# Expert stages of a two-layer gated cross-attention model: inner weights of groups 1 to 7 loaded in place, their low parts on GpSimd

## The reference

```python
# layer 0: E = 4 experts, D = 512, F = 2048, top 2 of 4
h = silu(einsum('td,edf->etf', xf, w1)) * einsum('td,edf->etf', xf, w3)
out = einsum('te,etd->td', gates, einsum('etf,efd->etd', h, w2))
# layer 1: E = 8 experts, D = 512, H = 1024, top 2 of 8
h1 = einsum('bsd,hd->bsh', x, W1[e]); h2 = einsum('bsd,hd->bsh', x, W2[e])
y = einsum('bsh,dh->bsd', h1 * sigmoid(h1) * h2, W3[e])
out = out + y * w_e[..., None]          # for e in range(8)
```

## Time and profile before

| | us |
|---|---|
| median of 3 runs (2252.22 to 2254.47) | 2253.94 |
| the profiled execution | 2267.11 |
| its span | 2265.1 |
| busy: PE / PEld / DVE / ACT / POOL | 1964.1 / 1589.4 / 1071.3 / 851.7 / 585.7 |

### The profile page before, as it was taken

How to read it: one execution, slowest core, us unless ns; L and a number is a source line. 1 busy time by engine, 2 the same in 40 slices (tenths; PEclk the granted TensorE clock), 3 DMA queues, 4 the chain that set the end, 5 groups by cost and what they waited for, 6 DMA issues and landing times. The chain is left out here.

```text
span 2265.1 us, 35412 instructions
## 1 busy us (share of the span) xinstructions
PE 1964.1 (87%) x12328; PEld 1589.4 (70%) x12328; DVE 1071.3 (47%) x2316; ACT 851.7 (38%) x1791; POOL 585.7 (26%) x479
## 2 busy tenths in 40 slices
PE   5799999999999999996699999999758667887883
PEld 3478777777878787875577877777537556776772
DVE  6325555555555555444544333333256644454444
ACT  3234343434434343343433333333134434444440
POOL 3030202020111111000433333434402044455453
PEclk9899999999999999998799999999878778999997
DMA  8620111010101020000433223333480333344445
GB/s 206 211 83 27 29 33 34 27 40 9 58 8 58 9 58 8 17 16 31 158 94 111 84 80 97 110 99 106 175 265 8 132 111 116 121 148 142 123 126 191
DMA packets 112954, 201.48 MB, mean 89 GB/s; under 512 B 32568, under 2 KB 33368, under 8 KB 112300
## 3 DMA queue, kind: packets, MB, share of 16 engines
q1 hardware_dynamic: 107196, 178.88, 26.0%
q0 software_dynamic: 4800, 15.73, 2.0%
q10 hardware_dynamic: 816, 5.05, 0.6%
HBM read 171.64 MB, written 27.98 MB: 88 GB/s over the span
## 5 line engine op out<-in xcount | busy, mean ns | idle before, releaser
L458 POOL TENSOR_TENSOR a_rows<-a_rows,a_gain_x 128x512 f32<-128x512 f32 (+1 forms) x48 | 68.2, 1420 | 555.4 <-DVE a_rows L873 555.4
L1090 PE MATMUL f_banks<-f_wab_hi,f_x_hi 128*128 x448 | 187.7, 419 | 18.0 <-DVE f_wab_lo L1670 10.8
L617 PE MATMUL a_kv_ps<-a_kvin_hi,a_wk_hi 128*128 128x512 f32 (+1 forms) x512 | 196.2, 383 | 1.0 <-DVE a_kvin_lo L880 1.0
L1090 PE MATMUL m_banks<-m_wab_hi,m_x_hi 128*128 x512 | 164.9, 322 | 36.6 <-DVE m_wab_lo L1670 24.5
L618 PE MATMUL a_kv_ps<-a_kvin_lo,a_wk_hi 128*128 128x512 f32 (+1 forms) x512 | 180.4, 352 | 0.0
L619 PE MATMUL a_kv_ps<-a_kvin_hi,a_wk_lo 128*128 128x512 f32 (+1 forms) x512 | 180.3, 352 | 0.0
L1092 PE MATMUL f_banks<-f_wab_hi,f_x_lo 128*128 x448 | 178.2, 398 | 0.0
L1091 PE MATMUL f_banks<-f_wab_lo,f_x_hi 128*128 x448 | 177.1, 395 | 0.0
L1709 DVE TENSOR_TENSOR f_h_sb<-f_h_sb,f_banks 128x256 f32<-128x256 f32 x112 | 47.2, 421 | 262.3 <-ACT f_h_sb L1445 258.9
L540 ACT ACTIVATE a_probs<-a_probs,a_neg_max 100x822 f32<-100x822 f32 x128 | 125.9, 984 | 113.1 <-DVE a_neg_max L904 112.9
L617 PE MATMUL a_kv_ps<-a_wv_hi,a_kvin_hi 128*128 128x512 f32 (+1 forms) x384 | 156.6, 408 | 1.0 <-DVE a_k_lo L897 1.0
(11 more groups left out here) (395 smaller groups left out, 4912.1 us busy)
## 6 DMA issues: line engine op xcount, KB each, us to landing
f_raw<-f_pieces SPq DMA_DIRECT2D x178, 256.0 KB, 2.8
m_raw<-m_pieces SPq DMA_DIRECT2D x176, 256.0 KB, 2.8
a_rows<-ctx SPq DMA_DIRECT2D x8, 1280.0 KB
ahead_piece<-g_ctx SPq DMA_DIRECT2D x3, 2880.0 KB, 26.3
a_wout_sb<-L_xattn_Wkv SPq DMA_DIRECT2D x8, 512.0 KB, 14.3
m_y_acc<-m_pieces SPq DMA_DIRECT2D x8, 512.0 KB, 7.1
f_y_acc<-f_pieces SPq DMA_DIRECT2D x7, 512.0 KB, 6.1
a_q_dram_hi<-a_qs_hi SPq DMA_DIRECT2D x2, 1600.0 KB, 8.5
```

Source lines behind the costliest of these rows:

```text
L458: own.link(nc.gpsimd.tensor_tensor(row, row, gain_x[0:n, :], ALU.mult))
L617: nc.tensor.matmul(out, hi_l, hi_r, start=first, stop=False)
L1090: nc.tensor.matmul(out, left_hi, right_hi, start=start, stop=False)
```

## The change

For groups 1 to 7 in both stages:

- Inner pieces 4 to 15 (`NEAR` = 4) no longer go through the ring. They are loaded in pairs, six DMAs of 512 KB, straight into the memory of `wab_lo`, under the name `wab_raw`, a tensor laid out at the same address. ScalarE reads the raw value there for the high part, and GpSimd subtracts in place. SyncE issues the six DMAs together, once all the inner parts of the group before are done. Pieces 0 to 3 and the outer pieces 16 to 23 stay in the ring of four (`ringed`).
- GpSimd makes all 24 low parts of these groups; VectorE makes none.
- TensorE waits, ahead of each slot's inner part, for the low parts up to that slot's expert (`PER` = 4 pieces an expert in f, 2 in m), with a count worked out from the expert's register, and no longer for all 16 ahead of the first slot.

Group 0 and the memory laid out are as before.

```diff
 class ExpertTensors:
         self.wab_hi = sb("wab_hi", [P, E, KD, 2 * FG], F32R)
+        with ExitStack() as early:
+            self.wab_raw = sb("wab_raw", [P, E, KD, 2 * FG], where=early)
         self.wab_lo = sb("wab_lo", [P, E, KD, 2 * FG], F32R)
...
-    SHARED = (2, 5, 7, 10, 13, 15)
+    NEAR = 4
+    PER = LAST // E
+    PAIR = 2
...
         def by_dve(g, c):
-            return c < LAST if g == 0 else c in SHARED
+            return g == 0 and c < LAST
...
+        def in_place(n):
+            return n >= PIECES and NEAR <= n % PIECES < LAST
 
         def raw_of(q, n):
             if q == 0 and n < DIRECT:
                 return y_acc[:, n, :]
-            return raw[:, (n - DIRECT * (1 - q)) % RING, :]
+            if in_place(n):
+                return split_dst(tensors.wab_raw, None, n % PIECES)
+            return raw[:, ringed[q].index(n) % RING, :]
...
             def load(q, n):
                 g, c = divmod(n, PIECES)
-                slot = n - DIRECT * (1 - q)
+                if in_place(n):
+                    if c == NEAR:
+                        sp.wait_ge(h_ready[q], SIZE[q] * g)
+                    if (c - NEAR) % PAIR == 0:
+                        to = tensors.wab_raw[:, :, :, :].rearrange("p e k f -> p (e k f)")[:, BANK * c:BANK * (c + PAIR)].rearrange("p (c d) -> p c d", d=D)
+                        sp.dma_start(to, pieces[g, c:c + PAIR, :, :].rearrange("c p d -> p c d")).then_inc(place_loaded[(c - NEAR) // PAIR][q], 16)
+                    return
+                slot = ringed[q].index(n)
                 if slot >= RING:
-                    wait_low(sp, q, *divmod(n - RING, PIECES))
+                    wait_low(sp, q, *divmod(ringed[q][slot - RING], PIECES))
...
                 with pe.Fori(0, G - 1) as i:
-                    pe.wait_ge(wlo_pool[q], LOW0 + POOL_FIRST + POOL_LOWS * i + LAST - DVE_LOWS)
-                    pe.wait_ge(wlo_dve[q], LOW0 + DVE_FIRST + DVE_LOWS + DVE_LOWS * i)
                     g = i + 1
                     for s in range(size):
+                        pe.wait_ge(wlo_pool[q], LOW0 + POOL_FIRST + PER + PIECES * i + PER * experts[s])
                         hidden(q, g, s, experts[s])
                         if s:
                             turn_hidden(q, g, s - 1)
-                    pe.wait_ge(wlo_pool[q], LOW0 + POOL_FIRST + POOL_LOWS + POOL_LOWS * i)
+                    pe.wait_ge(wlo_pool[q], LOW0 + POOL_FIRST + PIECES + PIECES * i)
...
-                given = 0
                 for s in range(size):
                     add(q, g, s)
-                    if g + 1 < G:
-                        due = len(SHARED) * (s + 1) // size
-                        for c in SHARED[given:due]:
-                            split(q, g + 1, c)
-                        given = due
```

More of the change, by code:

```diff
@@ L1249, in gated_experts @@
         raw_loaded = [both(f"raw_loaded{n}") for n in range(RING)]
+        place_loaded = [both(f"place_loaded{n}") for n in range((LAST - NEAR) // PAIR)]
         st_ready, xhi_done, xlo_done = both("st_ready"), both("xhi_done"), both("xlo_done")
@@ L1273, in gated_experts @@
         POOL_FIRST, DVE_FIRST = PIECES - LAST, LAST
-        POOL_LOWS, DVE_LOWS = PIECES - len(SHARED), len(SHARED)
         def wait_low(eng, q, g, c):
             eng.wait_ge((wlo_pool, wlo_dve)[by_dve(g, c)][q], LOW0 + low_count[g, c])
+        ringed = [[], []]
+        for q in range(2):
+            for n in range(DIRECT * (1 - q), G * PIECES):
+                if n < PIECES or not NEAR <= n % PIECES < LAST:
+                    ringed[q].append(n)
+        def in_place(n):
+            return n >= PIECES and NEAR <= n % PIECES < LAST
         def raw_of(q, n):
@@ L1289, in wait_raw @@
                 eng.wait_ge(direct_loaded[n // 2], 16)
+            elif in_place(n):
+                g, c = divmod(n, PIECES)
+                eng.wait_ge(place_loaded[(c - NEAR) // PAIR][q], 16 * g)
             else:
-                turn, slot = divmod(n - DIRECT * (1 - q), RING)
+                turn, slot = divmod(ringed[q].index(n), RING)
                 eng.wait_ge(raw_loaded[slot][q], 16 * (turn + 1))
```

## The result

| | us, median | runs |
|---|---|---|
| before | 2254.2 | 2252.22 to 2254.78 |
| after | 2161.4 | 2160.63 to 2167.09 |

The ratio is 0.9595, 95% interval 0.9578 to 0.9613: 92.8 us are gained. The forecast was 2179 us with a range of 2165 to 2214.

The account below looks back on a forecast made before the run. VectorE's low parts and adds delaying TensorE, chiefly in m, were taken as the bound. m's rounds 66.6, m's group 0 4.5 and f 10.8, less 3 and 4, gave 75 us: profiled 2267.1 to 2192, median 2179; range 2165 to 2214.

Parts of the forecast that it names:

- The 24.5 and the 27.7 us: Stage m: TensorE's inner matmuls wait 24.5 us for VectorE's low parts, outer ones 27.7 for its adds; one cause claimed.
- TensorE's round of 36.2 us: Stage m's loop: a round with no wait and no cold start takes 36.2 us, down from 47.8.
- three arrival times: After m's inner part ends (T0): sixth pair lands by 11.2 us, ScalarE free at 12.3, GpSimd's 16 low parts done at 22.5.
- The burst: Six paired loads issued at T0 + 0.3: first pair after 4.1 us, each further one 1.35 us later.
- The row of 26.3 us: Earlier 2880 KB load taking 26.3 us; basis of the late-burst rival, 2283 us, slower than before, 3%.
- The wait per expert: Before each slot's inner part: TensorE isn't held up by GpSimd; if it failed, m's rounds 47 us, total 2245, 2%.
- the third rival: Loop branch in f and m: waits for code, 3 us at 12 starts, 36 us less gained, 2212 us; 6%.
- the sum: Both stages' gains less added costs: 66.6 + 4.5 + 10.8 - 3 - 4 = 75 us.
- 12 starts at 0.25: Round starts in f and m: 0.25 us each charged for the branch and the wait, 3 us.
- 210 slots at 0.02: TensorE's slots in both stages: one added register instruction and wait each, 0.02 us charged, 4 us in all.
- Cold starts: TensorE at 1.2 GHz after long gaps: m's first round still begins cold, keeping about 3 us; clock 1.00 from the second.
- a wait of 4.5: m's group 0, outer part: the 4.5 us wait for L1699 goes as VectorE's low parts go.

## Why the prediction was right, and why it was too high

**What bounded m.** Right. The 24.5 and the 27.7 us went together, and the kernel with VectorE's low parts back has both again (18.9 and 20.5), while the one with one wait and no low part on VectorE has none ahead of the outer matmuls.

**TensorE's round of 36.2 us.** Right: 36.09. That it was the length to expect, and not one set by ScalarE or GpSimd, rested on three arrival times, all met within 0.5 us (T0 + 10.8, 11.95 and 22.05).

**The burst.** Right, taken from the earlier trace rows as the same shape from the same memory. The row of 26.3 us was rightly given little weight: the sixth pair was in ScalarE's hands 10.8 us after the first issue.

**The wait per expert.** Right in kind: with one wait instead, the gain is gone. The price was put too low: 66 us on top of 2179, where 2261.1 - 2161.4 = 100 were measured. My 47.3 us for the round left out that a gap of 10 us brings a cold start; it was 48.7. And f paid too, 65.5 against 61.7.

**Code at the branch.** Right against the third rival. The two matmuls on either side of the branch start 0.24 us apart. In the profile's list of DMA queues, q8 moved three packets in m's first round (1867 to 1906 us) and none in the rounds from 1906 to 2085 us, where q14 moved seven small ones, as in the earlier trace rows. That q8 carries TensorE's code is inferred: it rests in the rounds in which TensorE goes through the same loop again; the profile doesn't name the engine. The rule of the Trainium skill ("Runtime: NRT & Kernel Launch", section "Instruction fetch mechanics"), that a taken branch beyond the two pages held stops execution for a fetch, doesn't show here: no branch of the loop cost time.

**Where the 18 us lie.** Forecast and result differ by 2179 - 2161.4 = 17.6, or, in the terms of the sum, 93.2 - 75 = 18. No mechanism was wrong in kind. The step that failed is the sum of what is gained: it took off 7 us, for 12 starts and 210 slots, where the runs show 0, and it put m's group 7 at nothing, where the profile shows 3.2 us. The other errors of size point the same way, and single executions add a little:

| term | foreseen | measured | more |
|---|---|---|---|
| rounds of f and m | 69.6 - 3 + 10.8 = 77.4 | 13.5 + 68.1 = 81.6 | 4.2 |
| 12 starts at 0.25 | -3 | 0 (0.24 us from start to start) | 3 |
| 210 slots at 0.02 | -4 | 0 (24.5 us with half a wait, one, two) | 4 |
| m's group 0, outer part | 4.5 | 6.0 | 1.5 |
| m's group 7 | not counted | 3.2 | 3.2 |
| f's group 0 | not counted | 2.4 | 2.4 |

1. *The charges for the wait.* I charged for operations that no row shows, "so I take half of this", as part would lie behind the matmuls. All of it did. The value in the middle of the bounds was a hedge; the row nearest to it was the earlier trace rows, a slot at the pace of its matmuls with some ten register instructions in it already. That such instructions can cost something was not wrong: four more a slot cost 2192.0 - 2161.4 = 31 us, in m's inner parts (7 x 4.1 us).

2. *Cold starts.* I charged the first round's, and in the other five counted a cold start as gone. But group 7 starts cold too in the kernel before (a granted clock of 0.50 in its first 4 us), and its inner part, behind the last round, fell from 2216.39 - 2189.23 = 27.16 to 2110.67 - 2086.17 = 24.50 us. The first outer matmul of m's group 7, before and after:

```profile
2216.39 0.48 PE L1090 MATMUL m_banks<-m_wy_hi,m_ht_hi 128*128 x1
```

```profile
2110.67 0.48 PE L1090 MATMUL m_banks<-m_wy_hi,m_ht_hi 128*128 x1
```

I counted rounds from start to start and stopped one inner part short. In f, group 3 of the kernel before had started cold too (a clock of 0.57 in its first 4 us), though group 2 had not, after a longer gap (2.54 us, a clock of 1.00). Group 3's inner part took 1350.38 - 1307.18 = 43.2 us where its neighbours took 41.6. That is 1.6 of the 2.7 us by which f's rounds gained more than 10.8; the other 1.0 is that an idle time is counted from the modelled end of a matmul, and a round from start to start. In m the cold start that I left in the first round cost 38.12 - 36.09 = 2.0 us and not 3.

3. *Group 0.* m's outer part gained 6.0 where I read a wait of 4.5; 0.8 of the rest is the gap of the reads, 9.18 us in place of 10.02. f's group 0 was not in the sum; its 2.4 us lie in the inner part, which took 48.6, 51.4 and 52.6 us in three profiles of kernels that don't differ there, and so are the scatter of single executions.

4. *The range.* Its low end, 2165, had the two charges undone, 7 us, and some 6 for a shorter gap ahead of m's group 1, of which 0.8 came. Group 7's cold start and that in f could only add to the gain, and had no place in the range: a bound from below has to ask which stretches the sum doesn't cover. With the 2.7 us of group 7's cold start and the 1.6 in f taken off 2165 it would have stood near 2161, just below the result.

What I got by luck: in the profiled execution 13.1 us were the stall in group 0. Scaling from that execution to the median by the difference of their totals, 13 us, was right only because the stall lay in a stretch where the sum had no term.

## What to carry to other kernels

When one engine's split of weights gates another's start, let the consumer wait piece by piece in the order in which it will use them: here the faster loads and the move of the low parts to one engine were worth nothing together without that wait, and 93 us with it. Count a sum over a loop to the end of the last pass, not to its last start, and look at the clock behind each gap that goes. A register instruction added between matmuls was free here up to a threshold: look whether the slot runs at the pace of its matmuls, and test with several at once and with one.

## What the runs showed of the hardware

- An extra register instruction with a satisfied wait cost TensorE nothing in f's slots (4 more in a slot of 2.97 us), nothing in m's up to two a slot (1.54 us from slot to slot), and with five 0.26 us a slot in the mean of an inner part (28.6 in place of 24.5 us).
- Six paired loads of 512 KB each to one core came at one per 1.35 us, 388 GB/s, while TensorE, ScalarE and, from the first 2 us on, VectorE and GpSimd were at work.
- VectorE and GpSimd disturbed each other when both made low parts at the same time: VectorE's low part took 1.83 us instead of 0.68, GpSimd's up to 1.82 instead of 1.29. VectorE's adds, which read a bank and `y_acc`, left GpSimd at 1.30, 1.35 at most. The Trainium skill ("SBUF — State Buffer", section "SBUF: two separate sides") describes a port pair that a VectorE operation with two operands in that memory and one of GpSimd hold in turn; the rows agree, the adds having only one operand there.
- ScalarE stood still for 9 to 11 us ahead of one instruction in 3 of 11 profiles, always at the second silu of stage m, in the kernel before and in two variants of the changed one.
